# Edges on 128 partitions instead of 125, and the target-order tables built between the scatters

## What is computed

```python
h = relu(layernorm(x)); x = x + segment_sum((h @ W)[dst] * edge_weight, src) + b
h = relu(layernorm(x)); x = x + h + z_in[in_deg] + z_out[out_deg] + sigmoid(..) + sigmoid(..) \
                              + segment_sum(edge_attr @ W_sum + b_sum, src)
h = relu(layernorm(x)); x = x + attention_block(h, src, dst, edge_weight)   # softmax over the edges of a target
h = relu(layernorm(x)); x = x + gru(segment_sum(h[src] + rel[edge_type], dst), h)
```

## Time and profile before

| | us |
|---|---|
| median of 3 runs | 5610.76 |
| lowest, highest | 5604.88, 5611.56 |
| the profiled execution, its own time | 5615.93 |
| its span, first to last instruction | 5614.1 |
| VectorE busy, whole span | 3950.7 (70%) |
| GpSimd busy, whole span | 3898.1 (69%) |
| TensorE busy, whole span | 3530.3 (63%) |
| `prepare`, from the start to SP's first instruction of the next stage | 1475.6 |

### The profile page before, as it was taken

How to read it: one execution, slowest core, us unless ns; L and a number is a source line. 1 busy time by engine, 2 the same in 40 slices (tenths; PEclk the granted TensorE clock), 3 DMA queues, 4 the chain that set the end, 5 groups by cost and what they waited for, 6 DMA issues and landing times. The chain is left out here.

```text
span 5614.1 us, 108115 instructions
## 1 busy us (share of the span) xinstructions
PE 3530.3 (63%) x16558; PEld 2634.7 (47%) x16559; DVE 3950.7 (70%) x14077; ACT 1757.7 (31%) x6303; POOL 3898.1 (69%) x4332
## 2 busy tenths in 40 slices
PE   0000035200277777776768999999989778888887
PEld 0000012100255555554547888888879644554444
DVE  9918999300477777774568888888868766666665
ACT  0000000000133333332337777777756411111111
POOL 2878887776477777775766666666647777676774
PEclk9999999999999999997879999999999889899998
DMA  2232233335355555554323333333322233333332
GB/s 75 76 84 79 76 82 88 87 88 125 76 156 157 157 158 155 157 157 93 94 86 96 94 94 94 95 94 95 94 66 66 88 111 114 103 110 106 108 108 78
DMA packets 491102, 578.41 MB, mean 103 GB/s; under 512 B 114758, under 2 KB 394328, under 8 KB 490945
## 3 DMA queue, kind: packets, MB, share of 16 engines
q0 software_dynamic: 189536, 397.34, 25.4%
q1 hardware_dynamic: 301473, 180.10, 11.8%
HBM read 491.28 MB, written 86.57 MB: 103 GB/s over the span
## 5 line engine op out<-in xcount | busy, mean ns | idle before, releaser
L410 POOL DMA_INDIRECT src_records<-rec,pos_slot x800 | 1005.0, 1256 | 345.2 <-issue 237.0
L1289 POOL DMA_INDIRECT a_row<-h_rows,a_idx x832 | 787.6, 947 | 369.8 <-PE a_p_s L1415 197.1
L1905 POOL DMA_INDIRECT r_row<-h_rows,r_idx x832 | 802.1, 964 | 310.2 <-issue 168.2
L782 POOL DMA_INDIRECT s_row<-h_rows,s_idx x832 | 794.5, 955 | 299.7 <-issue 171.7
L794 PE MATMUL s_sums<-s_row,s_hotw 128*128 128x256 f32 x1664 | 584.9, 434 | 329.8 <-DMA s_row<-h_rows,s_idx 231.7
L1946 PE MATMUL r_p_s<-r_row,r_hot 128*128 128x272 f32 x1664 | 602.2, 474 | 233.2 <-DVE r_row L2080 215.1
L1392 PE MATMUL a_p_q<-nodes,a_hotT 128*128 x1664 | 569.8, 424 | 55.5 <-DVE a_score L1459 54.1
L1946 PEld LDWEIGHTS r_p_s<-r_row,r_hot 128*128 128x128 f32 x1664 | 335.4, 221 | 516.8 <-DVE r_row L2080 233.8
L820 DVE TENSOR_TENSOR nodes<-nodes,s_sums 128x385 f32 x832 | 461.5, 555 | 157.1 <-PE s_sums L795 138.7
L1415 PE MATMUL a_p_s<-a_row,a_masked 128*128 128x257 f32 x1664 | 497.0, 380 | 2.1 <-DVE sums L1496 1.4
L794 PEld LDWEIGHTS s_sums<-s_row,s_hotw 128*128 128x128 f32 x1664 | 253.0, 192 | 477.1 <-issue 369.6
(11 more groups left out here) (308 smaller groups left out, 8747.5 us busy)
## 6 DMA issues: line engine op xcount, KB each, us to landing
s_rec<-src_records SPq DMA_DIRECT2D x832, 66.0 KB
rec<-in_edge_attr SPq DMA_DIRECT2D x100, 500.0 KB
s_row<-h_rows,s_idx POOLq DMA_INDIRECT x832
a_row<-h_rows,a_idx POOLq DMA_INDIRECT x832, 2.8
r_row<-h_rows,r_idx POOLq DMA_INDIRECT x832, 2.8
src_records<-rec,pos_slot POOLq DMA_INDIRECT x800
h_rows<-H SPq DMA_DIRECT2D x1, 6272.0 KB
x_rows<-nodes SPq DMA_DIRECT2D x49, 128.0 KB, 1.9
```

The lines of the kernel that those rows point to most:

```text
L410: gp.indirect_dma_start(out=src_records, out_offset=bass.IndirectOffsetOnAxis(ap=pos_slot[:, k:k + 1], axis=0), in_=rec[:, k, :], in_offse ...
L782: gp.indirect_dma_start(out=row[:, k, :], out_offset=None, in_=env["h0_rows"], in_offset=bass.IndirectOffsetOnAxis(ap=idx[:, k:k + 1], axis=0)
L1289: gp.indirect_dma_start(out=row[:, k, 0:D], out_offset=None, in_=env["h2_rows"], in_offset=bass.IndirectOffsetOnAxis(ap=idx[:, k:k + 1], a ...
L1905: gp.indirect_dma_start(out=row[:, k % R, 0:D], out_offset=None, in_=env["h3_rows"], in_offset=bass.IndirectOffsetOnAxis(ap=idx[:, k:k + 1 ...
```

## The change

- `EP` becomes 128 and `STEPS` 784: 49 turns, 784 scatters of 128 rows. The last partition holds 432 real edges; its other 352 steps point at spare rows behind the records. A DMA over the edges is split in three: partitions 0 to 111, 112 to 126, and 127 alone. From turn 27 on the last one is left out.
- The four copies into `by_dst` and the padding rows move to SP's queue, ahead of the loop of loads.
- `windows` gets two buffers. GpSimd issues the gathers of chunk 0 before turn 34 of the scatters, and those of chunks 1 to 6 two turns apart; a chunk waits for the casts of the chunk two before. VectorE's `hots` are cut into seven parts, one ahead of each chunk.
- SP stores the small tables before the loads of turn 34, and issues the 6.4 MB store of `H` before the loads of turn 40.
- In `source_sums`, `s_nbase` comes before the clearing of `nodes`, and ScalarE waits for `s_nbase` only.

```diff
-EP = 125
-STEPS = EDGES // EP
+EP = 128
+STEPS = -(-EDGES // (EP * 16)) * 16
+LAST_STEPS = EDGES - (EP - 1) * STEPS
+SPARE = STEPS - LAST_STEPS
+FULL = 112
...
+    LAST_TURNS = LAST_STEPS // (2 * HALF)
+    WIN_TURN, WIN_APART = 34, 2
+    STORE_TURN = 40
+    HOT_TURNS = STEPS // (8 * CHUNKS)
...
-        windows = sb(ctx, "windows", [P, 4, P], I32)
+        windows = sb(ctx, "windows", [P, 2, 4, P], I32)
...
             def _(sp):
-                def load(turn, h):
-                    sp.dma_start(rec[:, h * HALF:(h + 1) * HALF, 0:ED],
-                                 attr[:, bass.ds(turn * 2 * HALF + h * HALF, HALF), :]
-                                 ).then_inc(rec_loaded[h], 16)
+                def load(turn, h, last):
+                    steps = bass.ds(turn * 2 * HALF + h * HALF, HALF)
+                    ks = slice(h * HALF, (h + 1) * HALF)
+                    sp.dma_start(rec[0:FULL, ks, 0:ED], rows[0][:, steps, :]).then_inc(rec_loaded[h], 16)
+                    sp.dma_start(rec[FULL:EP - 1, ks, 0:ED], rows[1][:, steps, :]).then_inc(rec_loaded[h], 16)
+                    if last:
+                        sp.dma_start(rec[EP - 1:EP, ks, 0:ED], rows[2][:, steps, :]).then_inc(rec_loaded[h], 16)
...
+                for n, name in (("src", "src"), ("dst", "dst"), ("wgt", "edge_weight"), ("typ", "edge_type_16")):
+                    sp.dma_start(by_dst[n][0:EDGES, :].rearrange("(a b) o -> a (b o)", a=32),
+                                 A[name].rearrange("(a b) -> a b", a=32)).then_inc(dst_copied, 16)
...
+                loads(1, LAST_TURNS, True)
+                loads(LAST_TURNS, WIN_TURN, False)
                 sp.wait_ge(tables_ready, 2)
                 for n, t in (("sb", blk_i["src"]), ("ss", start_i["src"]), ("db", blk_i["dst"])):
...
+                loads(WIN_TURN, STORE_TURN, False)
                 sp.wait_ge(tables_stored, 48)
...
+                sp.wait_ge(h0_ready, BLOCKS)
+                sp.dma_start(env["h0_rows"].rearrange("(i p) d -> p i d", p=P), H[:]).then_inc(h0_stored, 16)
+                loads(STORE_TURN, REC_TURNS, False)
...
             def _(gp):
-                scatters((FIRST_PAIR, REC_TURNS))
-                for h in range(2):
-                    gp.wait_ge(rec_stored[h], STEPS // (2 * HALF) * 16 * HALF)
+                scatters((FIRST_PAIR, WIN_TURN))
...
                 for ch in range(CHUNKS):
-                    if ch:
-                        gp.wait_ge(win_cast, ch)
+                    if ch >= 2:
+                        gp.wait_ge(win_cast, ch - 1)
...
+                    first = WIN_TURN + ch * WIN_APART
+                    scatters((first, first + WIN_APART if ch < CHUNKS - 1 else REC_TURNS))
+                for h in range(2):
+                    gp.wait_ge(rec_stored[h], STEPS // (2 * HALF) * 16 * HALF)
...
             def _(ac):
-                ac.wait_ge(cleared, 2)
+                ac.wait_ge(based, 1)
...
             def _(ve):
+                ve.wait_ge(tables, 48)
+                nc.vector.tensor_scalar(nbase[:], blk_all[:], -float(P), None, ALU.mult).then_inc(based, 1)
                 nc.vector.memset(acc[:], 0.0).then_inc(cleared, 1)
```

More of the change, by code:

```diff
@@ new lines, in _ @@
+                attr = A["edge_attr_128"]
+                rows = [attr[a * STEPS:b * STEPS, :].rearrange("(p t) d -> p t d", t=STEPS) for a, b in ((0, FULL), (FULL, EP - 1))]
+                rows.append(attr[(EP - 1) * STEPS:EDGES, :].rearrange("(p t) d -> p t d", p=1))
+                def load(turn, h, last):
[5 more added lines that the diff above has]
+                        sp.dma_start(rec[EP - 1:EP, ks, 0:ED], rows[2][:, steps, :]).then_inc(rec_loaded[h], 16)
@@ L352, in _ @@
                 for h in range(2):
-                    load(0, h)
+                    load(0, h, True)
                 sp.wait_ge(rel_pad, 1)
@@ L372, in _, with loads @@
                     sp.dma_start(by_dst[n][EDGES:EDGES + P, :], t).then_inc(tail_stored, 16)
+                for n, name in (("src", "src"), ("dst", "dst"), ("wgt", "edge_weight"), ("typ", "edge_type_16")):
+                    sp.dma_start(by_dst[n][0:EDGES, :].rearrange("(a b) o -> a (b o)", a=32),
+                                 A[name].rearrange("(a b) -> a b", a=32)).then_inc(dst_copied, 16)
+                def loads(first, end, last):
+                    with sp.Fori(first, end) as turn:
+                        for h in range(2):
+                            sp.wait_ge(rec_stored[h], turn * (16 * HALF))
+                            load(turn, h, last)
+                loads(1, LAST_TURNS, True)
+                loads(LAST_TURNS, WIN_TURN, False)
                 sp.wait_ge(tables_ready, 2)
@@ L474, in complete @@
                         ks = slice(h * HALF, (h + 1) * HALF)
-                        ac.wait_ge(rec_loaded[h], turn * 16 + 16)
+                        if last:
+                            ac.wait_ge(rec_loaded[h], turn * 48 + 48)
+                        else:
+                            ac.wait_ge(rec_loaded[h], turn * 32 + (LAST_TURNS * 16 + 32))
                         ac.wait_ge(ranked_steps, step + HALF)
@@ L496, in _ @@
                 with ac.Fori(FIRST_PAIR + PAIRS, REC_TURNS) as turn:
-                    complete(turn)
+                    complete(turn, False)
             @block.tensor
@@ L516, in _ @@
                 degrees(0, True)
-                with pe.Fori(1, STEPS // 8) as turn:
-                    degrees(turn, False)
                 for ch in range(CHUNKS):
+                    with pe.Fori(max(1, ch * HOT_TURNS), (ch + 1) * HOT_TURNS) as turn:
+                        degrees(turn, False)
                     pe.wait_ge(win_cast, ch + 1)
@@ L694, in _ @@
                 hots(0, True)
-                with ve.Fori(1, STEPS // 8) as turn:
-                    hots(turn, False)
-                ve.wait_ge(hot_used, STEPS)
-                nc.vector.tensor_copy(c["indeg"][:], p_deg[:])
                 for ch in range(CHUNKS):
-                    ve.wait_ge(win_loaded, 64 * (ch + 1))
+                    with ve.Fori(max(1, ch * HOT_TURNS), (ch + 1) * HOT_TURNS) as turn:
+                        hots(turn, False)
+                    ve.wait_ge(win_loaded[ch % 2], 64 * (ch // 2 + 1))
                     if ch:
```

97 lines of the change are left out of this document (56 added, 41 removed).

## The result

The changed kernel takes 5367.15 us (median of 4 runs, 5360.29 to 5377.04) against 5611.16 for the one before on the same chip: 244.0 us less, a ratio of 0.9567 (95% interval 0.9548 to 0.9585). 5360 was forecast. The profiled execution took 5377.04 us, its span 5375.2. Against the span of before, 5614.1, that is 238.9 less: `prepare` 252.2 less, the stages between 1.6 less, the last stage 14.9 more.

A forecast was written before the change was run, and what follows sets the result against it. GpSimd's scatter issue was taken as the bound up to 1380.5 us, then a serial chain of 95.1 us. `prepare` -247 and the next stage -4 gave -251: from 5610.76 to 5360, range 5320 to 5550 with some 85%.

The forecast's parts named there:

- The scatter: GpSimd's scatters in `prepare`: 128 rows need 0.955 us undisturbed instead of 1.181, with 32 to 48 packets each.
- the dear case: Rival, 18%: a scatter of 128 rows stays as dear as one of 125; 5544 us, up to 23 more.
- The disturbance: Scatters beside VectorE's rank segments: each keeps some 0.205 us extra, a pace of 1.47 us instead of 1.26.
- From the first scatter behind `rstd` (379.6) to chunk 0: `prepare`'s middle: scatters resume at 390.5 us after the wait for `rstd`, and turn 34 with the first chunk comes at 868.
- The loads: Loads refilling a half: landing 4.2 us after issue, a chain of 6.8 us, hidden behind the other half's 10.1.
- The case against them: Rival: loads get no faster and bind the free pace, costing 36 us, 5396; 9% together with a scatter price in between.
- The stall: Store of `H` before turn 40's loads: GpSimd waits 9.4 us, taken as 10, bounded by 0 and 25.
- The tables: Small tables stored before turn 34's loads: 21.3 us against 25.2 that GpSimd still has to issue, so no stall.
- The loop starts and the test: Seven loop starts and the load and test of `fall_i`, among the late scatters: 10 us for all eight together.
- The last scatter: End of GpSimd's scatters in `prepare`: 868+302+35+10+10 = 1225 us.
- The end of `prepare`: From the last scatter's end to the next stage: 2.3 us landing and 1.0 barrier, so the stage starts at 1228.3.
- The next stage: Start of `source_sums`: `s_nbase` first brings gathers some 10 us earlier, clearing starts 1 us later; gain 4, bounded by 0 and 11.

The follow-up runs named there:

- e1: Changed kernel plus, per half, eight scratch scatters of 127 to 64 rows and, per chunk, spare gathers of 125 and 112 rows; 6586.52 us, run once.
- e4: Changed kernel with the attribute loads cut at partition 125 instead of 112; 5421.17 us, ratio 0.9666.
- e2: Kernel before with only the 128-row shape, split loads and the new start of the next stage, in the old order; 5393.85 us, ratio 0.9614.
- e3: Changed kernel's order and start of the next stage, but 125 rows, 800 steps and whole loads as before; 5590.24 us, ratio 0.9962.
- e9: Changed kernel with the clearing of `nodes` in pieces, first seven blocks ahead, the other 42 in turns 1 to 6; 5348.86 us, ratio 0.9530.
- e10: Changed kernel run once more without an edit; 5367.09 us, ratio 0.9566.

## Why the prediction was right, and where not

- **The scatter** (0.955 us, 31.8 packets): right, and the step that carried the result. Its median over all scatters is 0.969 to 0.972 us, and 0.965 to 0.970 is the mean where nothing disturbs it. The packets did tell the two shapes apart; e1 excludes that rows or direction set the price, the main reason for the 18% of the dear case.
- **The disturbance** was mis-sized: 0.205 us was kept, 130.16/123 = 1.058 and 184.65/167 = 1.106 against 0.965 undisturbed give 0.09 to 0.14. Up to 281 us 123 scatters were done instead of 113, two of them by the earlier start (112.2, not 115), and `rstd` came at 369.5 instead of 380.5.
- **From the first scatter behind `rstd` (379.6) to chunk 0** 478.2 us passed, 477.5 were forecast. Two errors cancel: less disturbance beside the target ranks, but 1.28 instead of 1.26 in the rest. This agreement is luck. Chunk 0 stood at 857.8 (868).
- **The loads**: landing 4.9 us after issue (4.2), hidden. The case against them was real and dearer than written: 54 us in e4 instead of 36, with the longer issue of e4's second piece in it.
- **The stall** at turn 40: 10.1 us (9.4, taken as 10). The size is right, but not its parts: SP was held for 11.2 us instead of 27.3, and the load of 994 had landed only 18.3 us after its issue.
- **The tables** were forecast without a stall, and that step failed: GpSimd stood for 3.6 us, and for 4.4 in the second execution of the same kernel. SP was held for 0.40, 1.18 and 1.89 us, not for 14.5; the wait came through the scatters, which landed late beside the tables' small packets. No run moves the tables alone; e2, which has them behind the last scatter, doesn't have the wait.
- **The loop starts and the test** of `fall_i` had 10 us. From chunk 0 to the end of the last scatter 355.9 us passed; 240 scatters at 1.275, 28 gathers at 1.26 and the two stalls leave less than 2 for them. So this term was too large, and it covered the tables' stall.
- **The last scatter** ended at 1213.7 (1225): the 11 us are those of `rstd`.
- **The end of `prepare`** was mis-sized: 9.7 us from the last scatter's end to the next stage, 3.3 were forecast. The data had landed by 1214.7, so the landing is no cause. In e3 it was 6.0. The 9.3 us that stand behind the last scatter before are as long and were read as landing and test. But there the DMA engines were 94% busy, with SP's stores for the most part, and still moved 351 packets of scatters, so the two waits needn't be the same. What fills the 9.7 us is open.
- **The next stage** failed as a step: -4 forecast, none measured. Its last gather starts 1086.6 us after the stage's start, 1086.4 before, and 1082.7 to 1090.1 in the other runs with the new start and a whole clearing. What failed is that the clearing "starts 1 us later": behind `s_nbase`, which waits for a load, it starts 4.6 us later. e9 shows that the clearing was on the path: cut into pieces, it gives 7.6 us of the stage.
- **The last stage**, 14.9 us longer in the profile and 8.4 in e10's, is a term that the prediction didn't have.

Sum in the profile: forecast -247 for `prepare` and -4 behind it; measured -252.2, -1.6 and +14.9. The mechanism, the cheap scatter, is right and shown; that the forecast was only 7 us off is in part luck, since terms of 5 to 15 us cancel.

## What to carry to other kernels

For an indirect DMA, look at its packets per instruction and at the divisors of its row count before anything else: padding 125 rows to 128 took 18% off GpSimd's time for each of 800 instructions and was worth 216 us, the reordering 20 alone and 27 behind it. When the engine that sets the pace gets faster, work out the chain that refills its buffers again, since its cover shrinks with the pace; here loads in the shape of before (125 partitions in one piece, two beside it) took 54 of the 244 us. A big clearing on a path is better cut into pieces between the work that uses it than moved as a whole; for the store the same took the stall away, with a gain that isn't clear of the noise. Look also at small stores: three tables of 3.5 KB each, in packets under 512 B, cost a wait of 3.6 to 8.2 us.

## What was unexpected in the hardware

- A scatter of 127 rows costs GpSimd 2.55 us, one of 126 rows 0.99, one of 128 rows 0.97, one of 64 rows 0.92.
- VectorE's rank segments slow a scatter of 128 rows by 0.09 to 0.14 us and one of 125 rows by 0.205.
- Three tables of 3.5 KB in packets under 512 B delayed the next load by 11 us, and GpSimd waited 3.6 to 8.2 us for it.
- The last stage takes 1162.5 to 1178.8 us at granted clocks of 0.83 to 0.93 (quarters of the stage), and 6.5 us apart in two profiled executions of the same program.
- Between the last scatter's end and the next stage 6.0 (e3) to 9.7 us pass where nothing else is under way, and for 4.5 to 8.7 us of it no engine and no DMA is busy.
